# Decoder layer on one core: more fp32 matmuls replaced by sums of fp16 parts, and the attention rows accumulated in PSUM

## What is computed

```python
x = layernorm(x + attn(x))                 # q, k, v = x @ W_qkv.T + b; rope on q and k; softmax(q k / sqrt 32) v
Q, K, V = x @ Wq.T, ctx @ Wk.T, ctx @ Wv.T # by heads
Ks, Vs = tree(K), tree(V)                  # 9 levels; K: mean of a pair, V: sum of a pair; 1023 nodes
nk, nv = Ks[idx_table], Vs[idx_table]      # 12 nodes for each of the 512 rows, the same table in each batch
w = softmax([Q.K, Q.nk (masked)] / sqrt 32)
x = layernorm(x + (w . [V, nv]) @ Wo.T + bo)
x = layernorm(x + relu(x @ w1 + b1) @ w2 + b2)
```

## Time and profile before

| what | before |
|---|---|
| median of 3 runs (lowest, highest) | 2490.13 us (2486.86, 2492.05) |
| the profiled execution's own time | 2490.27 us |
| its span, first to last instruction | 2488.4 us |
| mean granted TensorE clock | 0.950 |
| busy share of the span: PE, DVE, ACT, POOL | 87%, 71%, 31%, 43% |
| DMA, mean over the span | 153 GB/s |

### The profile page before, as it was taken

One profiled execution on the slowest core, in us unless ns is written; L12 is line 12 of the kernel. 1 busy time (PEld: TensorE's weight loads), 2 busy tenths in 40 slices (PEclk: granted clock), 3 DMA queues, 4 the chain that ended last, 5 costly groups with the idle time before them and its releaser, 6 DMA issues.

```text
span 2488.4 us, 31001 instructions
## 1 busy us (share of the span) xinstructions
PE 2160.1 (87%) x9824; PEld 1030.9 (41%) x9824; DVE 1774.8 (71%) x2321; ACT 772.8 (31%) x1143; POOL 1062.4 (43%) x1108
## 2 busy tenths in 40 slices
PE   5899999999999999981368999889998899988997
PEld 2333333333333333320134555445554455544554
DVE  7555646474756656445798988988889888888950
ACT  3344444444544444550011211112122121221221
POOL 3232423332414233214545556465565645546531
PEclk9999999999999999995689999999999999999999
DMA  6333424243432433227756556564655646556510
GB/s 204 114 119 97 133 67 133 74 136 94 135 104 94 128 103 118 73 73 258 271 185 224 167 200 208 172 225 157 217 188 184 221 160 222 182 193 210 173 67 20
DMA packets 175789, 379.72 MB, mean 153 GB/s; under 512 B 19748, under 2 KB 69028, under 8 KB 175656
## 3 DMA queue, kind: packets, MB, share of 16 engines
q0 software_dynamic: 55296, 201.35, 23.2%
q1 hardware_dynamic: 120360, 176.85, 22.0%
HBM read 306.57 MB, written 71.30 MB: 152 GB/s over the span
## 4 chain that ended last, share of the span: by engine, by line
issue 19%; DVE 18%; DMA 8%; POOL 5%; PE 4%; DVEq 0%; POOLq 0%; ACT 0%; SPq 0%
DMA nb<-kv_flat,idx_rows 7%; DVE logits L1279 4%; POOL nb L1458 3%; DVE nb L1329 2%; PE bank L1096 2%; DVE nb L1270 2%; POOL nb L1486 1%; DVE o_sb L1342 1%; PE bank L1084 1%; DMA own<-kv_flat 1%; DVE stats L1369 1%; DVE nb L1337 1%; DVE x L1367 1%; DVE own L1274 1%; DVE logits L1283 1%
## 5 line engine op out<-in xcount | busy, mean ns | idle before, releaser
L690 DVE TENSOR_REDUCE neg_max<-rows_ps 128x2 f32<-128x1024 f32 x256 | 312.6, 1221 | 314.3 <-PE rows_ps L485 313.4
L1096 PE MATMUL bank<-w_sb,hid 128*128 128x512 f32 x1024 | 513.3, 626 | 0.0
L1458 POOL DMA_INDIRECT nb<-kv_flat,idx_rows x384 | 390.2, 1016 | 156.5 <-issue 101.9
L1208 ACT ACTIVATE hid<-bank,b_sb 128x256 f32<-128x256 f32 x256 | 120.7, 471 | 770.4 <-PE bank L1084 722.8
L1270 DVE TENSOR_TENSOR nb<-nb,bank 128x1024 f32<-128x1024 f32 x192 | 230.9, 1219 | 128.2 <-DMA nb<-kv_flat,idx_rows 87.5
L610 ACT ACTIVATE probsT<-e_ps 128x1024 f32<-128x1024 f32 x256 | 261.9, 1023 | 168.4 <-PE e_ps L513 168.0
L1084 PE MATMUL bank<-x2T_hi,w_hi_sb 128*128 128x256 f16 x1024 | 282.1, 275 | 15.9 <-DVE x2T_lo L1377 15.9
L1084 PE MATMUL bank<-x2T_lo,w_hi_sb 128*128 128x256 f16 x1024 | 281.5, 275 | 0.0
L1084 PE MATMUL bank<-x2T_hi,w_lo_sb 128*128 128x256 f16 x1024 | 281.1, 274 | 0.0
L503 PE MATMUL o_ps<-probsT,v_sb 128*33 128x512 f32 x1024 | 272.9, 611 | 6.3 <-ACT oT L607 6.1
L1486 POOL TENSOR_TENSOR nb<-nb,weights 128x1024 f32<-128x1024 f32 x96 | 197.3, 2069 | 157.4 <-DVE weights L1316 156.7
(11 more groups left out here) (123 smaller groups left out, 2992.2 us busy)
## 6 DMA issues: line engine op xcount, KB each, us to landing
kv_flat<-kv_nat SPq DMA_DIRECT2D x128, 256.0 KB, 2.6
own<-kv_flat SPq DMA_DIRECT2D x32, 512.0 KB
q_stack<-qk_dram SPq DMA_DIRECT2D x96, 128.0 KB, 2.7
k_stack<-qk_dram SPq DMA_DIRECT2D x96, 128.0 KB, 3.1
in_sb<-in_xT SPq DMA_DIRECT2D x8, 1024.0 KB, 6.4
in_sb<-in_ctxT SPq DMA_DIRECT2D x8, 1024.0 KB, 6.6
qk_dram<-hi SPq DMA_DIRECT2D x32, 256.0 KB, 2.2
qk_dram<-lo SPq DMA_DIRECT2D x32, 256.0 KB, 2.7
```

The costliest lines, as they stand in the source:

```text
L690: dve.tensor_reduce(neg_max[:, g % 2, at:at + 2], rows_ps[:], AX.X, ALU.max, negate=True).then_inc(max_done, 1)
L1096: mm = pe.matmul(ACC[i][:], hid[:, c % 2, i * P:(i + 1) * P], w2_sb[:, c, :], start=False, stop=c == WC - 1)
L1458: pool.indirect_dma_start(nb[:, slot(lt, g), k, :], None, kv_flat, bass.IndirectOffsetOnAxis(idx_rows[:, lt, at:at + 1], 0))\
```

## The change

Those three products of the second phase are made of fp16 parts too, three fp16 matmuls for each fp32 one. Wq, Wo and w2 go through the same splitting in the first phase as w1 (40 pieces, five in each batch, steps 5, 11, 17, 23, 29), and are loaded as hi and lo parts in the second phase. For the moving side, a low part has to be made of what is in PSUM: ACT copies the bank as fp16 (hi), PE adds minus hi to the same bank with one matmul against minus the identity (`turn_minus_hi`, `hidden_minus_hi`), and ACT copies what is left (lo). For the hidden rows, hi is made slightly too small (DOWN), so that the rest stays positive under the relu. This takes `split_x2` off DVE. Attention rows are accumulated in a PSUM bank, O, which is the bank of PROJ: `pair` is gone, each of the 12 weighted rows is added to O by itself, and ACT copies O to o_sb for PE (`copy_o`). Turns of o and x1 stand one or two chunks earlier and each projection one chunk after its turn. Scalings by 64 are undone in ACT's and DVE's last steps.

```diff
-W1_LOAD, W1_SPLIT, W1_STORE = (5, 22), (8, 25), (11, 28)
+PIECE_LOAD, PIECE_SPLIT, PIECE_STORE = (2, 8, 14, 20, 26), (5, 11, 17, 23, 29), (7, 13, 19, 25, 31)
-OUT_AT, QUERY_AT, EXP_AT, APPLY_AT, X2_AT = (2, 11), (3, 10), (4, 12), (5, 13), (6, 14)
+OUT_AT, QUERY_AT, EXP_AT, APPLY_AT, X2_AT = (1, 9), (2, 8), (4, 12), (5, 13), (6, 14)
...
                         if d in PIECE_SPLIT:
                             n = b * EACH + PIECE_SPLIT.index(d)
                             act.wait_ge(piece_loaded, START + n * 16 + 16)
                             act.wait_ge(piece_stored, START + n * 32)
                             act.activation(piece[:], piece[:], ACT.Copy, scale=W_UP).then_inc(piece_hi_done, 1)
                             act.wait_ge(piece_hi_done, START + 2 * n + 1)
                             act.activation(piece_hi[:], piece[:], ACT.Copy).then_inc(piece_hi_done, 1)
...
-            TURN, PROJ, HB, ACC, Q = bank[0], bank[1], bank[2:4], bank[4:6], bank[6:8]
+            TURN, PROJ, O, HB, ACC, Q = bank[0], bank[1], bank[1], bank[2:4], bank[4:6], bank[6:8]
...
+                def turn_minus_hi(b, lt, kind):
+                    take_hi(turn_of(b, lt, kind))
...
+                    pe.matmul(TURN[:], minus_one[:], hi, start=False, stop=True, skip_group_check=True)\
+                        .then_inc(turn_rest, 1)
+                def times(o, lt, kind, w, start):
+                    slot_ = ACT_SLOT[kind, lt % RT]
+                    for c in range(KC):
+                        for i, (x_part, w_part) in enumerate(((actT_hi, w[0]), (actT_hi, w[1]), (actT_lo, w[0]))):
+                            mm = pe.matmul(o, x_part[:, slot_, c, :], w_part[:, c, :], start=start and c + i == 0,
+                                           stop=c == KC - 1 and i == 2)
+                    return mm
+                def hidden_minus_hi(b, half, c):
+                    pe.wait_ge(h_hi_done, START + (b * 2 + half) * WC + c + 1)
+                    pe.matmul(HB[c % 2][:, 0:RW], minus_up[:], hid_hi[:, c % 2, :], start=False, stop=True,
+                              skip_group_check=True)\
+                        .then_inc(h_rest, 1)
...
-                        mm = pe.matmul(ACC[i][:], hid[:, c % 2, i * P:(i + 1) * P], w2_sb[:, c, :],
-                                       start=False, stop=c == WC - 1)
+                        for k, (h_part, w) in enumerate(((hid_hi, w2_sb[0]), (hid_hi, w2_sb[1]), (hid_lo, w2_sb[0]))):
+                            mm = pe.matmul(ACC[i][:], h_part[:, c % 2, i * P:(i + 1) * P], w[:, c, :],
+                                           start=False, stop=c == WC - 1 and k == 2)
...
+                def turned_parts(b, lt, kind, hi, lo):
+                    number = turn_of(b, lt, kind)
+                    src = TURN[:].rearrange("p (c t) -> p c t", c=KC)
+                    act.wait_ge(turn_ready, START + number + 1)
+                    act.activation(hi, src, ACT.Copy).then_inc(turn_hi_done, 1)
+                    act.wait_ge(turn_rest, START + number + 1)
+                    act.activation(lo, src, ACT.Copy).then_inc(turn_copied, 1)
+                def copy_o(b, lt):
+                    act.wait_ge(o_part, START + (b * TT + lt + 1) * O_STEPS)
+                    act.activation(o_sb[:, lt % 2, :], O[:], ACT.Copy).then_inc(o_copied, 1)
...
+                        act.activation(hid_hi[:, c % 2, :], HB[c % 2][:, 0:RW], ACT.Relu, scale=DOWN / W_UP,
+                                       bias=b1_down[:, c:c + 1]).then_inc(h_hi_done, 1)
...
+                        act.wait_ge(h_rest, START + n + 1)
+                        act.activation(hid_lo[:, c % 2, :], HB[c % 2][:, 0:RW], ACT.Relu, scale=1.0 / W_UP,
+                                       bias=b1_sb[:, c:c + 1]).then_inc(h_ready, 1)
...
-                        dve.tensor_tensor(v[:, 0, :], v[:, 0, :], v[:, 1, :], ALU.add).then_inc(v_pair, 1)
-                        dve.tensor_tensor(o, o, nb[:, slot(lt, g), 0, D:2 * D], ALU.add).then_inc(o_part, 1)
+                    def accumulate(g, k):
+                        dve.wait_ge(o_part, START + n * O_STEPS + 1 + g * GN + k)
+                        dve.tensor_tensor(O[:], O[:], nb[:, slot(lt, g), k, D:2 * D], ALU.add).then_inc(o_part, 1)
...
-                        accumulate(g)
+                        accumulate(g, 0)
                         if g + 1 in DVE_V_GROUPS:
                             multiply(g + 1)
+                        accumulate(g, 1)
...
-                dve.tensor_tensor(x2T_lo[:, :, lt * P:(lt + 1) * P],
-                                      TURN[:].rearrange("p (c t) -> p c t", c=KC),
-                                      x2T_hi[:, :, lt * P:(lt + 1) * P], ALU.subtract).then_inc(x2_split, 1)
```

More of the change, by code:

```diff
@@ L1004, in _ @@
                 load_x1(0, 1)
-                sp.dma_start(wq_sb[:], chunks(wqT)).then_inc(consts2, 16)
+                for dst, part in zip(wq_sb, parts):
+                    sp.dma_start(dst[:], chunks(part[WQ_AT * P:WO_AT * P, :])).then_inc(consts2, 16)
                 for i, v in enumerate((bo, b2)):
@@ L1065, in project_out @@
                     pe.matmul(PROJ[:], ones_rows[:], bias_rows[:, 0, :], start=True, stop=False)
-                    for c in range(KC):
-                        mm = pe.matmul(PROJ[:], actT[:, ACT_SLOT["o", lt % RT], c, :], wo_sb[:, c, :],
-                                       start=False, stop=c == KC - 1)
-                    mm.then_inc(proj_ready, 1)
+                    times(PROJ[:], lt, "o", wo_sb, False).then_inc(proj_ready, 1)
                 def project_query(b, lt):
@@ L1074, in project_query @@
                         pe.wait_ge(v_mul_dve, START + (b * TT + lt - 1) * len(DVE_V_GROUPS))
-                    for c in range(KC):
-                        mm = pe.matmul(Q[lt % RT][:], actT[:, ACT_SLOT["q", lt % RT], c, :], wq_sb[:, c, :],
-                                       start=c == 0, stop=c == KC - 1)
-                    mm.then_inc(q_ready, 1)
+                    times(Q[lt % RT][:], lt, "q", wq_sb, True).then_inc(q_ready, 1)
                 def hidden(b, half, c):
@@ L1105, in mlp @@
                     first, second = ah * RT, ah * RT + 1
-                    pe.wait_ge(x2_split, START + b * TT + half * RT + RT)
+                    pe.wait_ge(turn_copied, START + turn_of(b, half * RT + 1, "x") + 1)
                     hidden(b, half, 0)
+                    hidden_minus_hi(b, half, 0)
                     for c in range(1, WC):
                         hidden(b, half, c)
+                        if attend and c == OUT_AT[0] + 1:
+                            project_out(ab, first)
+                        if more and c == QUERY_AT[0] + 1:
+                            project_query(qb, qh * RT)
+                        if more and c == QUERY_AT[1] + 1:
+                            project_query(qb, qh * RT + 1)
+                        if attend and c == OUT_AT[1] + 1:
+                            project_out(ab, second)
                         if attend and c == OUT_AT[0]:
@@ L1230, in mlp @@
                             turned_x2(ab, second)
+                        act.wait_ge(h_rest, START + n + 1)
+                        act.activation(hid_lo[:, c % 2, :], HB[c % 2][:, 0:RW], ACT.Relu, scale=1.0 / W_UP,
+                                       bias=b1_sb[:, c:c + 1]).then_inc(h_ready, 1)
+                        if attend and c + 1 == OUT_AT[0]:
+                            copy_o(ab, first)
+                        if attend and c + 1 == OUT_AT[1]:
+                            copy_o(ab, second)
                     if after_first and attend:
@@ L1236, in _ @@
                 exponentials(0, 0)
+                copy_o(0, 0)
                 turned(0, 0, "o")
@@ L1329, in multiply @@
                         dve.tensor_tensor(vv, vv, w, ALU.mult).then_inc(v_mul_dve, 1)
-                    def pair(g):
+                    def accumulate(g, k):
+                        dve.wait_ge(o_part, START + n * O_STEPS + 1 + g * GN + k)
+                        dve.tensor_tensor(O[:], O[:], nb[:, slot(lt, g), k, D:2 * D], ALU.add).then_inc(o_part, 1)
+                    multiply(0)
+                    if not (isinstance(b, int) and b == 0 and lt == 0):
+                        dve.wait_ge(o_copied, START + n)
+                    dve.tensor_tensor(O[:].rearrange("p (h d) -> p h d", h=H),
+                                      own[:, D:2 * D].rearrange("p (h d) -> p h d", h=H),
+                                      w_ps[:, NN, :].unsqueeze(2).to_broadcast([P, H, DH]), ALU.mult)\
+                        .then_inc(o_part, 1)
+                    for g in range(NG):
                         if g in POOL_V_GROUPS:
```

212 lines of the change are left out of this document (116 added, 96 removed).

## The result

The changed kernel takes **2435.88 us** (median of 4 runs, 2432.43 to 2437.57), the kernel before 2489.03 beside it (4 runs, 2486.86 to 2492.05): a ratio of 0.9784, 95% interval 0.9772 to 0.9796, 53 us less. The forecast was 2428 with a range of 2398 to 2474. The profiled execution's span fell from 2488.4 to 2432.9 us, 55.5 less, at a mean clock of 0.937 (0.950 before).

What follows compares the result with a forecast made beforehand. PE was taken to bound the first phase, the DVE, POOL and DMA tile loop the second. 2490.3 - 62 (tile path) - 4 (end) + 4 (first phase) = 2428 us, range 2398 to 2474.

Steps and rivals of the forecast that it cites:

- The path of a tile: Second phase: weights, POOL's multiplies, group 0 in O, gathers, landing, keys; 2.0 us a tile earlier, 62 us less over 31.
- Its links: Within a tile: adds 0.72 us apart, POOL's multiplies 3.84 us, first gather 0.9 earlier, gathers' issue another 0.7 + 0.4.
- the landing sets the keys: Rival, 7%: gathers' landing, not POOL's issue, sets when keys are ready; issue-to-use time grows from 5.2 us, total 2490.
- the adds into O are dear: Rival, 15%: PSUM adds cost 1.05 us a step, values take 4 us longer, a tile gains only 0.7 us: 2468.
- Worth nothing: Second phase: fp16 products cut PE's round from 70.8 to 65.0 us, but only become PE waiting until the last tile.
- the same bytes: Start of second phase: weight loads unchanged in bytes, w2 in 1 KB rows; counted 0, between -5 and +5 us.
- First phase and start: First phase: 24 more pieces cost 0.5 us a batch, 4 us in all; start of the second phase 0.
- The end: After DVE's last values, PE alone sets the time; the last 18 chunks save 0.32 us each, less two stalls: 4 us.
- PE's waits: Second phase: PE stands waiting 8.8 us a round of two tiles instead of 7.0.
- DVE's wait before the key multiply: Second phase, before the key multiply: DVE's wait grows by 0.3, to about 4 us a tile.
- The clock rival: Rival, 6%: PE's growing gaps lower its clock in the second phase; 30% of work at 1.2 GHz gives 2597 us.

Runs made afterwards that it cites:

- the kernel with PE relieved: Kernel before with only the attention rows accumulated in PSUM, and a third of the hidden layer's products left out: 2438.53 us, ratio 0.9780.
- The fp16 parts alone: Changed kernel with all products as sums of fp16 parts, but attention rows multiplied, paired and added in SBUF as before: 2483.76 us, ratio 0.9958.
- the rows-alone kernel: Kernel before with only the attention rows added one by one into PSUM bank O; products stay fp32, split_x2 stays on DVE: 2470.47 us, ratio 0.9908.
- the run with the later turn: Changed kernel with the output's turn one hidden-layer step later (steps 2 and 10 for 1 and 9, first query at 3): 2429.92 us, ratio 0.9743.
- the run with group 5 on DVE: Changed kernel with row group 5 multiplied by DVE, POOL keeping groups 3 and 4 only: 2503.23 us, ratio 1.0045.
- the late work: Changed kernel with three idle bn_stats a tile on DVE, 1.87 us together, at the end of the values: 2445.94 us, ratio 0.9828.
- own rows first: Changed kernel with the load of tile 1's own rows issued ahead of the two loads of w2: 2449.62 us, ratio 0.9806.
- The kernel with more work on PE: Changed kernel with three extra 256-column fp16 matmuls in each hidden chunk, overwritten by the next product: 2447.29 us, ratio 0.9821.
- early work: Changed kernel with three idle bn_stats a tile on DVE, 1.87 us together, ahead of group 0 in O: 2474.05 us, ratio 0.9914.
- own rows first and the later turn: Changed kernel with tile 1's own rows loaded ahead of w2 and the output turned one hidden-layer step later: 2450.34 us, ratio 0.9827.

## Why the prediction was right, and where it was not

**The path of a tile** was right as a mechanism and too large as a number. 2.0 us were forecast and 1.87 measured, but only 1.4 of these are the rows' own (the kernel with PE relieved), 42 us of the 62. Its links came as worked out: adds 0.73 us apart (0.72 forecast), POOL's two multiplies 3.78 (3.84), first gather 0.77 us earlier (0.9), eight gathers 1.86 earlier (2.0). What the sum left out is the landing: the rival "the landing sets the keys", given 7%, took part with 0.7 us of 1.9 in the tile shown. The intervals of the four places in a batch shrank by 1.5, 2.8, 1.2 and 1.9 us. The 2.8 are not all the path's: in that interval the kernel before has a second stop of DVE on "issue", 1.2 to 1.8 us, which the changed kernel lacks (last section), so the three others, 1.5 in the mean, are the fairer measure, and they agree with the 1.4. That the total came so near is in part luck: no term of the sum had DVE's second stop. That the adds into O are dear is excluded, and neither the product into O (685 to 690 ns over 32 tiles) nor the adds (692 to 700 ns over 384) were held up by POOL.

**"Worth nothing" for the fp16 products on PE** is the step that failed, though the total did not show it. The 62 us were booked on the rows in PSUM; alone these give 23. The prediction's own numbers left PE 70.8 us of work in a round of 73.8 without the fp16 products, so 3 us of room; at the faster pace PE also waited 67 us between turns and products, 5 us a round, which the sum had at nothing. With PE relieved the tiles give back 21 us. The fp16 parts alone are indeed worth nothing in the 25 ordinary intervals (38.06 against 38.13), but the rows need PE's room to give their gain. The sum came out because the change brings both together.

**The first interval** was missing from the sum: 3.7 us. A load that is issued behind w2's two was costed as "the same bytes". That explains it only in part: the rows-alone kernel, which loads w2 in one transfer, already takes 46.4 us there against 44.4.

**First phase and start**: 4 + 0 forecast. PE's busy time there is unchanged (925.68 against 925.96), and the first product came 1.4 us earlier: nothing to pay.

**The end**: 4 us forecast, 1.7 measured. DVE's last x2 waits 8.8 us for PE, 9.8 before.

**PE's waits**: 8.8 us a round forecast; the four rows above make 140 us in 14.5 rounds, 9.7. DVE's wait before the key multiply, both rows of it as in the forecast: from 101.7 to 109.7 us in 1070, 3.8 us a tile where 4 was forecast.

**The clock rival** (6%): the granted clock did fall, from 0.96 to 0.93 in this window, and the run with the later turn shows that it cost nothing in the tiles. In the run with group 5 on DVE a gap of PE, half the clock after it, and DVE's wait for the late product stand one behind the other; how much of the 67 us is the clock's, no run separates.

Term by term, for the 55.5 us between the profiled spans: 1.4 - 3.7 + 56.1 + 1.7. Forecast: -4 + 62 + 4.

## What to carry over

Before a term is called worth nothing because an engine has slack, put the slack against the new pace: add the engine's busy time and the waits that its own order forces on it, and compare with the shorter round. A half of a change can look weak alone (23 us of 53) when a second engine is nearly full, and worth nothing is then not the same as not needed. An interval-by-interval list of one landmark instruction shows in a minute what totals hide: here one late load, and, once a batch, a stop of 5 us at a loop's start.

## What was not expected of the hardware

**Code is fetched again at the start of a loop iteration, and the engine stands still for it.** DVE's line "issue" (waiting for nothing that the profile shows) is five waits of 4.5 to 5.1 us between 1330 and 2400 us. One of them, with the DMA view of the microseconds around it:

```profile
1838.88 2.35 DVE L1358 TENSOR_TENSOR nb<-nb,bank 128x1024 f32<-128x1024 f32 x2 [4.96 <-issue]
```

```profile
q14 instruction: 1, 0.01, 0.4%
```

They lie 148 to 149 us apart, at the first key multiply behind the loop's branch. In all five a packet of 8 KB on that queue starts 2.0 us before DVE goes on. That the queue carries DVE's code is concluded from runs in which only DVE's code differs, below. The kernel before has ten such waits in five iterations, a long and a short one each, with a packet 1.8 to 2.1 us ahead. The two kernels with three operations a tile added on DVE have neither: between 1500 and 2250 us their queue 14 shows 1 packet, where the kernel before and the changed one show 25, and their issue waits are short. DVE's issue wait with the late work, against the 23.9 of the changed kernel:

```profile
DVE nb L1361 <- issue: 5.7, 14, 1.1
```

PE does the same from time to time. This is the start of the stretched interval of 43.8 us in the run with own rows first, and then its code packets between 1500 and 2250 us:

```profile
1864.02 0.38 PE L1136 MATMUL bank<-w_hi_sb,hid_lo 128*128 128x512 f16 x1
1868.55 0.39 PE L1117 MATMUL bank<-x2T_hi,w_hi_sb 128*128 128x256 f16 x1 [4.15 <-issue]
```

```profile
q8 instruction: 18, 0.29, 0.2%
```

Blocks of 16 KB start at 1861.6 and 1865.9; the other stretched interval has them at 2016.1 and 2020.5. The late-work run has 18 such packets too and gaps of 4.8 and 3.9 us in two of its three stretched intervals. The kernel with more work on PE has 45, and stops at every second round's start (2.7 to 4.7 us, six times). The kernel before and the repeated changed kernel have none in that stretch. But such a stop alone does not stretch an interval: the profiled changed kernel has one of 4.8 us at 1419.2, behind blocks at 1412.2 and 1416.6, in an interval of 37.5 us, and the six of the kernel with more work on PE lie in intervals of 36.4 to 38.4. The Trainium skill says of this (Runtime: NRT & Kernel Launch, on instruction fetch mechanics) that a taken branch to a block outside the buffered ones forces a fetch before execution goes on; the trace agrees, with 4.5 to 5.1 us each time on DVE in the changed kernel. It does not say why PE's loop is fetched again in some iterations and not in others, and no run here settled it. Nor was a loop with a shorter body tried on DVE, where five waits of nearly 5 us are in plain sight.

**Open.** Some kernels carry a sign that this study did not follow up: ACT's relu of a hidden chunk starts 1.2 to 10 us after the record of the product that it waits for. Between 1330 and 2350 us this happens at 26 places with the rows alone, 26 with early work, 25 with late work, 21 with own rows first, 25 with own rows first and the later turn, 14 with group 5 on DVE and 9 with the fp16 parts alone. It happens at two in the kernel before, and at none in the changed kernel, its repeat, the kernels with PE relieved or with more work, and those with the later turn and without own rows first. So the three kernels with scattered stretched intervals and the one that lost 67 us all have it, and no run shows whether it is their cause. PE's records may stand too early there: where the semaphore of that product is on record (1827.57 us with group 5 on DVE), it rose 4.8 us after the product's record ended. The gaps of PE at the start of an iteration in that run are of this kind. They have no code packet near them; that they go when the output is turned later is shown, why they arise is not. Of the stretched intervals of the last run with own rows first, the first has code blocks at 1406.0 and 1408.3 and a stop of PE of 2.6 us, and the two others have none. Why the fourth interval grew when DVE took group 5 along with the later turn is half seen: DVE stops there a second time, 2.3 to 3.0 us at L1367, with a packet of queue 14 1.8 us ahead of each.
